# Edge sums of a graph network: two operands of the VectorE work placed in PSUM

## What is computed

```python
# layer 0, attention with 8 heads; layer 3 is alike, with a loop edge for each node
e = leaky_relu(el[src] + er[dst]); e = exp(e - segment_max(e, dst)[dst])
msg = feat[src] * a[:, :, None]
out = segment_sum(msg, dst, num_segments=N)
# layer 1, with edge features of width 256 and one weight for each edge
msg = (node_feats[src] + edge_feats) @ W1.T + b1
agg = segment_sum(wbar[:, None] * msg, dst, num_segments=n)
```

## Time and profile before

| what | before |
|---|---|
| time, median of 3 runs | 6092.86 us (6085.9 to 6096.81) |
| the profiled execution: its time, its span | 6083.9 us, 6082.1 us |
| TensorE matmul busy (share of the span) | 4117.7 us (68%) |
| VectorE busy | 2744.4 us (45%) |
| ScalarE busy | 903.3 us (15%) |
| POOL busy | 1805.6 us (30%) |
| mean DMA rate | 121 GB/s |
| mean granted TensorE clock | 0.825 of full |
| `gat_sum`, `edge_sum`, `loops_sum` | about 610 to 968, 1862 to 2208, 5404 to 5740 us |

### The profile page before, as it was taken

One profiled execution on the slowest core, in us unless ns is written; L12 is line 12 of the kernel. 1 busy time (PEld: TensorE's weight loads), 2 busy tenths in 40 slices (PEclk: granted clock), 3 DMA queues, 4 the chain that ended last, 5 costly groups with the idle time before them and its releaser, 6 DMA issues. The chain is left out here.

```text
span 6082.1 us, 67316 instructions
## 1 busy us (share of the span) xinstructions
PE 4117.7 (68%) x18035; PEld 2867.8 (47%) x18037; DVE 2744.4 (45%) x6601; ACT 903.3 (15%) x1972; POOL 1805.6 (30%) x1518
## 2 busy tenths in 40 slices
PE   0582884456705676766898999989945826646539
PEld 0441553234404454533576766767635813334337
DVE  4664555325657565587102011020151255575558
ACT  0200001111000012127102021020222310000012
POOL 2465770226645730100000000000003056657400
PEclk9896886556957887898998999989957967878759
DMA  3364893224727830013542432414222225724300
GB/s 112 88 201 137 288 292 110 78 70 134 215 85 250 281 98 16 3 62 159 178 129 68 141 106 93 133 58 145 74 71 74 64 58 152 229 85 143 102 27 21
DMA packets 476269, 734.24 MB, mean 121 GB/s; under 512 B 67999, under 2 KB 349147, under 8 KB 471574
## 3 DMA queue, kind: packets, MB, share of 16 engines
q1 hardware_dynamic: 339515, 504.54, 25.9%
q0 software_dynamic: 81376, 175.99, 10.7%
q10 hardware_dynamic: 55154, 51.01, 2.5%
HBM read 594.23 MB, written 136.80 MB: 120 GB/s over the span
## 5 line engine op out<-in xcount | busy, mean ns | idle before, releaser
L744 PE MATMUL gin_up_sums<-gin_ring,gin_acc 125*128 125x250 f32 (+1 forms) x4000 | 1069.6, 427 | 23.0 <-ACTq L777 23.0
L744 PEld LDWEIGHTS gin_up_sums<-gin_ring,gin_acc 125*128 125x128 f32 x4000 | 755.7, 189 | 331.2 <-ACTq L777 24.0
L726 DVE BATCH_NORM_STATS2 gin_up_stat<-gin_mlp_z x160 | 77.8, 486 | 1160.5 <-ACT gin_mlp_z L774 1160.5
L2290 POOL IOTA two_seats_pid<- 125x1 f32 x1 | 0.1, 137 | 1616.8 <-ACTq L2287 1616.8
L2887 PE MATMUL edge_sum_part<-edge_ring_rows,edge_sum_hot 128*125 x832 | 237.1, 445 | 115.1 <-DVE edge_sum_hot L1687 55.5
L2887 PE MATMUL loops_sum_part<-loops_ring_rows,loops_sum_hot 128*125 x832 | 239.4, 452 | 98.3 <-DVE loops_ring_rows L1289 48.5
L3015 POOL DMA_INDIRECT edge_ring_rows<-edge_table,src_e x203 | 255.6, 1259 | 167.7 <-PE edge_sum_part L2887 111.9
L3245 PE MATMUL adj_counts_part<-adj_counts_far,adj_counts_low 128*128 128x325 bf16 x1032 | 209.4, 336 | 102.6 <-DVE adj_counts_far L3226 41.8
L3015 POOL DMA_INDIRECT gat_ring_rows<-gat_table,src_e x203 | 238.4, 1175 | 101.6 <-issue 55.8
L3015 POOL DMA_INDIRECT loops_ring_rows<-loops_table,src_e x203 | 236.9, 1167 | 105.1 <-issue 56.1
L2887 PEld LDWEIGHTS edge_sum_part<-edge_ring_rows,edge_sum_hot 128*125 128x125 f32 x832 | 178.1, 221 | 173.9 <-issue 141.0
(11 more groups left out here) (804 smaller groups left out, 7705.2 us busy)
## 6 DMA issues: line engine op xcount, KB each, us to landing
gin_ring<-gin_adj SPq DMA_DIRECT2D x100, 937.5 KB, 4.8
gin_ring<-gin_adj SPq DMA_DIRECT2D x100, 625.0 KB, 3.9
edge_sum_own<-edge_attr_in SPq DMA_DIRECT2D x97, 512.0 KB
gin_adj<-adj_counts_tile SPq DMA_DIRECT2D x25, 1562.5 KB
gat_sum_ef<-edge_attr_t_in SPq DMA_DIRECT2D x128, 256.0 KB
gat_gat_held<-edge_attr_t_in SPq DMA_DIRECT2D x64, 256.0 KB
pre<-gat_gat_held ACTq DMA_DIRECT2D x124, 128.0 KB
gat_ring_rows<-pre SPq DMA_DIRECT2D x31, 512.0 KB
```

Of the source, the lines that this page charges most:

```text
L726: v.bn_stats(statf[:, bass.ds(i * 12 + (h * 6 + f * UNITS * 6), 6)], z1f[:, nodes(i, h, f * N)]).then_inc(stats, 1)
L744: mm = pe.matmul(sums[h][k][:, 0:n * P].rearrange("p (t n) -> p t n", n=P), acc[:, t, k * 128:(k + 1) * 128], ring[0:P, q, 0:n, c * P:(c + ...
L2290: pool.iota(pid[:], pattern=[[0, 1]], base=0, channel_multiplier=1, allow_small_or_imprecise_dtypes=True).then_inc(made, 1)
```

## The change

Two things move to PSUM, which has two banks left in these stages. In all three stages a tile `numbers` there gets a copy of the numbers 0 to 124, and the one-hot instructions read it instead of `g.iota`. In the two stages of `sum_heads` a tile `scales` of 512 numbers for each partition gets blocks of the weights: 64 chunks at a time in `gat_sum` (8 weights an edge, 7 blocks in all), 32 in `loops_sum` (16 an edge, 13 blocks). Before a block is overwritten VectorE waits until its own earlier instructions on `msg_ready` have ended, and after it until the copy has ended. The copy of the weights into the rows and the product read `scales` instead of `weight`. The other operand of each instruction, and every output but those of the new copies, stay in SBUF. The sum in `sum_edges` (L1694) is as before.

```diff
 sum_heads:
+        numbers = st.ps("numbers", [EP, 512])
+        IN_PSUM, scales_in = 512 // WH, st.sem("scales_in")
+        scales = st.ps("scales", [EP, 512])[:].rearrange("p (c w) -> p c w", w=WH)
...
-                    make_hot(v, g, hot, s, j, summed, hot_ready)
-                    n = chunks_in(s, j)
+                    make_hot(v, numbers, g, hot, s, j, summed, hot_ready)
+                    n, c = chunks_in(s, j), s + j
                     if n:
                         k = j % RING
+                        if c % IN_PSUM == 0:
+                            many = min(IN_PSUM, C - c)
+                            if c > 0:
+                                v.wait_ge(msg_ready, 2 * c)
+                            v.tensor_copy(scales[:, 0:many, :], weight[:, c:c + many, :]).then_inc(scales_in, 1)
+                            v.wait_ge(scales_in, c // IN_PSUM + 2)
+                        w = c % IN_PSUM
                         ahead.wait_for_rows(v, loaded, ring, s, j)
-                        v.tensor_copy(rows[:, k:k + n, D:], weight[:, bass.ds(s + j, n), :]).then_inc(msg_ready, n)
+                        v.tensor_copy(rows[:, k:k + n, D:], scales[:, w:w + n, :]).then_inc(msg_ready, n)
                         msg = rows[:, k:k + n, 0:D].rearrange(by_head, h=H)
-                        v.tensor_tensor(msg, msg, weight[:, bass.ds(s + j, n), 0:H].unsqueeze(3).to_broadcast([EP, n, H, HD]), ALU.mult).then_inc(msg_ready, n)
+                        v.tensor_tensor(msg, msg, scales[:, w:w + n, 0:H].unsqueeze(3).to_broadcast([EP, n, H, HD]), ALU.mult).then_inc(msg_ready, n)
 
                 v.memset(zeros[:], 0.0).then_inc(empty, 1)
+                v.tensor_copy(numbers[:, 0:P], g.iota[0:EP, 0:P]).then_inc(scales_in, 1)
+                v.wait_ge(scales_in, 1)
                 for_quads(step)
...
 sum_edges:
+        numbers, numbered = st.ps("numbers", [EP, 512]), st.sem("numbered")
...
-                        v.tensor_scalar(hot[:, (j + n) % HOTS, :], g.iota[0:EP, 0:P], g.place_s[:, bass.ds(s + (j + n), 1)],
+                        v.tensor_scalar(hot[:, (j + n) % HOTS, :], numbers[:, 0:P], g.place_s[:, bass.ds(s + (j + n), 1)],
                                         mean[:, bass.ds(chunk, 1)], ALU.is_equal, ALU.mult).then_inc(hot_ready, 1)
...
+                v.tensor_copy(numbers[:, 0:P], g.iota[0:EP, 0:P]).then_inc(numbered, 1)
+                v.wait_ge(numbered, 1)
...
-def make_hot(v, g, hot, s, j, summed, hot_ready):
+def make_hot(v, numbers, g, hot, s, j, summed, hot_ready):
...
-    v.tensor_tensor(hot[:, k:k + QUAD, :], g.iota[0:EP, 0:P].unsqueeze(1).to_broadcast([EP, QUAD, P]),
+    v.tensor_tensor(hot[:, k:k + QUAD, :], numbers[:, 0:P].unsqueeze(1).to_broadcast([EP, QUAD, P]),
                     g.place_s[:, bass.ds(s + j, QUAD)].unsqueeze(2).to_broadcast([EP, QUAD, P]), ALU.is_equal).then_inc(hot_ready, QUAD)
```

## The result

The change makes the kernel a little slower: 6113.47 us median (6089.46 to 6123.82, 20 runs) against 6088.07 us for the kernel before on the same chips, a ratio of 1.0037 with a 95% interval of 1.0027 to 1.0046, some 22 us by the ratio (the medians lie 25 us apart). Forecast were 67.5 us less. The profiled execution of the changed kernel has a span of 6122.0 us at a mean granted clock of 0.822.

A forecast was written before the change was run, and what follows sets the result against it. POOL's gathers, held by VectorE instructions with two SBUF tensors, were taken to bound loops_sum and edge_sum, with gat_sum less clear. Terms -40 - 32 + 1.5 + 3 = -67.5 us took 6092.9 to 6025 us, range 6004 to 6064.

The forecast's parts named there:

- `loops_sum`, -40 us: Gathers of loops_sum: none held any more, POOL bounds the stage and nothing else is close, so 40 us less.
- `gat_sum`, -32 us: Gathers of gat_sum: unheld, but the DMA engines and TensorE follow closely, so 32 us less of at most 46.
- Rival 1: gat_sum is bound elsewhere than by POOL and gives only some 5 us; 6052 us in all, chance 0.17.
- One-hots of `edge_sum`, +1.5 us: Slower one-hots read from PSUM in edge_sum, 0 to 0.076 us each, mostly hidden under VectorE's waits: 1.5 us more.
- Rival 5: Slower: gathers still held, and edge_sum's slower PSUM one-hots lie on the path, 30 us more; 6127 us, chance 0.04.
- Blocks and numbers, +3 us: Copies of weight blocks and numbers to PSUM: mostly under waits, those ahead of each stage's first product cost 3 us.

The follow-up runs named there:

- hots_only: Changed kernel, but in sum_heads only one-hots and numbers come from PSUM; product and weight copy read SBUF again. Ratio to the kernel before 1.0020.
- before_rest: Kernel before, with POOL resting for one memset of 384 columns after each gathered quad in all three stages. Ratio to the kernel before 1.0045.
- heads_only: Changed kernel with the change in sum_heads alone; one-hots of edge_sum read SBUF again. Ratio to the kernel before 1.0012.
- before_quad: Kernel before, with TensorE counting its steps once for four instead of after each. Ratio to the kernel before 0.9985.
- rest_quad: Changed kernel, with POOL resting for one memset of 384 columns after each gathered quad in all three stages. Ratio to the kernel before 0.9994.
- plain_loads: Changed kernel, but SP issues 203 plain loads of neighbouring (wrong) rows in place of the gathers of loops_sum. Ratio to the kernel before 0.9800.
- after_hots32: Changed kernel, with VectorE allowed 32 one-hots ahead of TensorE in loops_sum, not 16. Ratio to the kernel before 1.0025; loops_sum 327.1 us.

## Why the prediction was wrong

**`loops_sum`, -40 us: wrong.** The step that failed is "POOL bounds this stage ... Next in line is TensorE with 239 of 336 us, at 416 steps 0.58 us a step ... I take 40, near the upper end, since nothing else is close." The 298 of 301 us were true, but a stage bound by POOL's gathers was taken for one in which everything else would run at its own pace if they were faster. What the runs showed in its place: the denser POOL gathers, the later TensorE's counts come. Late counts in `loops_sum` go from 26 to 130 us, and as POOL waits for them too, its 253 us of gathers still take 302 us. The stage is 201 us without gathers, 324 to 336 us with POOL's work at 253 to 298 us, and 356 us with the long rests. Nor are TensorE's 0.58 us a step a pace that it keeps beside the gathers: with 32 one-hots ahead, where it hardly waited for VectorE, it was 0.79. Measured: +2.2 us.

**`gat_sum`, -32 us: wrong, and by the same step.** The forecast dismissed VectorE's 49.2 + 40.0 us of waits for TensorE, "so TensorE keeps up". These waits were late counts already (65 us of them). Rival 1 had the place right and the mechanism not (it thought of the DMA engines). Measured: +4.2 us.

**One-hots of `edge_sum`, +1.5 us: wrong.** The price of each lay inside its bounds: 59 ns on the median (340 to 399 ns). The Trainium skill ("VectorE: DVE Perf Modes", section "Why PSUM operands drop a tier") has fp32 at the single rate with an operand in PSUM; an estimate from its rates is 65 ns, and the trace agrees within 6 ns on the median (in the mean 359 to 399 ns, 40 more). What failed is "VectorE waits 97.3 us in this stage ..., so this is hidden". Over all profiles whose POOL does not rest here, `edge_sum` takes 353.0 us on average with one-hots from PSUM (10 profiles, 341.6 to 361.0) and 341.7 us with them from SBUF (6 profiles, 339.7 to 344.0), 11 us more. Late counts are 16 to 63 us in the first and 0 to 17 us in the second group. Why slower one-hots that hold nothing bring more of them was not tried by itself. Rival 5 named the outcome, but also had the gathers of `sum_heads` still held, which they are not.

**Blocks and numbers, +3 us:** no run takes them out by themselves beside the gathers; without the gathers `loops_sum` alone is 8.1 us longer, mostly by the blocks.

**The sum.** The same averages give +11.0 us for `gat_sum` (357.9 in 8 profiles against 346.9 in 5, those with rests and `hots_only` aside) and +5.2 us for `loops_sum` (333.8 in 5 against 328.6 in 3), with +11.3 us for `edge_sum` 27.5 us together; the runs say 22 us. Single profiles of the two groups overlap or nearly touch (`gat_sum` 351.7 to 368.9 against 341.5 to 355.5, `loops_sum` 331.5 to 335.9 against 324.7 to 333.7). So the held gathers cost nothing as things stood. A hold of POOL is a rest in which TensorE gets through: the gather held for 23.2 us in `before_rest` shows it directly, and `hots_only` and the table of rests fit. Without the holds the same time and somewhat more goes into late counts.

**No version beats both clearly.** `best1` is `heads_only` with one rest a quad and counts by quads:

> Candidate to beat both: sum_edges as before (one-hots from SBUF), sum_heads as changed with one rest of POOL (384 columns) after each gathered quad, and TensorE counting once for four steps. From before_quad 0.9985, heads_only to rest_quad about 8 us less in the two stages: 0.996 to 1.000 of before. If late counts with whole quads weigh more than single ones, 1.000 to 1.003.

Measured: 1.0008 (0.9993 to 1.0023), level with before; late counts 113 us in `loops_sum`. Of the versions that compute the whole, only `before_quad` lies under the kernel before, 0.9985 (0.9971 to 0.9999), about 9 us, hardly more than its interval.

**Open.** Through what POOL's gathers slow TensorE: the runs exclude the number of counts, POOL's waiting on the semaphore, the traffic of rows, and the 16 one-hots, but `plain_loads` changed the issuing engine, the queue, the length of the packets and the making of descriptors at once, and did not take these apart. Nor was it tried to make the 203 gathers outside the stages, as is done with the other 124 chunks already; 130 us of `loops_sum` are at stake for that, less what the gathers and a further load cost elsewhere.

## What to carry to other kernels

When an engine is busy from end to end of a stage, that shows the bound for now, not what the others could do without it: before a gain is put at the full difference, run the stage once with that engine's work left out or done another way (here 201 and 336 us), and see what the neighbours' pace is then. The engine's own work has to be put back into that difference before any of it is called slowing (here 253 us of gathers, which leave some 50 us). Waits on a count whose producer has, by its records, long finished are a reading of their own; they stood in the trace of before. And a hold on one engine can be a rest that another lives on, so removing it is worth only what the next run shows.

## What the runs showed of the hardware

While POOL issues indirect DMAs one after another (0.945 us each, 0.30 us apart), the recorded updates of TensorE's count lie in a grid of about 0.7 us, and VectorE finds the counts up to 11.5 us late, and in bursts; with 32 one-hots ready TensorE's matmuls, too, start 1.4 us apart for a while (`after_hots32`). Three memsets' rest of 1.4 us after each four gathers ends the late counts in `loops_sum`; one of 0.46 us does not where no gather is held (109 us), and does where gathers are (`before_rest`). The same bytes loaded from SP's queue, 203 DMAs of 128 KB in 201 us at 217 GB/s, do nothing of the kind. A gather can be held over many VectorE instructions in a row: 23.2 us in `before_rest`, until the last of them. A VectorE operation with one of its inputs in PSUM never held a gather (406 of 406), and a gather beside it did not lengthen it (product 1207 ns).
